# Ranks of a graph kernel's edge sort from five partly added one-hot rows: one addition on VectorE and 16 products on TensorE in place of four and four

## The reference, cut to what matters

```python
def _spmm(row, col, val, h, n_nodes):
    return jax.ops.segment_sum(val[:, None] * h[col], row, num_segments=n_nodes)
output_low = jax.nn.relu(_spmm(row, col, val_low, x @ weight_low, n))
output_high = jax.nn.relu(_spmm(row, col, val_high, x @ weight_high, n))
```

## Time and profile before

| | |
|---|---|
| time, median of 3 runs | 2471.05 us (2466.08 to 2477.81) |
| the profiled execution: its time | 2489.27 us |
| the profiled execution: its span | 2487.5 us |
| PE busy, products | 1724.4 us (69%), 9081 instructions |
| DVE busy | 1253.1 us (50%), 3123 instructions |
| ACT busy | 895.6 us (36%), 2606 instructions |
| POOL busy | 1376.2 us (55%), 1351 instructions |
| mean granted clock of TensorE | 0.833 of full speed |

### The profile page before, as it was taken

How to read it: one execution, slowest core, us unless ns; L and a number is a source line. 1 busy time by engine, 2 the same in 40 slices (tenths; PEclk the granted TensorE clock), 3 DMA queues, 4 the chain that set the end, 5 groups by cost and what they waited for, 6 DMA issues and landing times.

```text
span 2487.5 us, 30925 instructions
## 1 busy us (share of the span) xinstructions
PE 1724.4 (69%) x9081; PEld 1439.1 (58%) x9081; DVE 1253.1 (50%) x3123; ACT 895.6 (36%) x2606; POOL 1376.2 (55%) x1351
## 2 busy tenths in 40 slices
PE   4788886998845257775776777777677577577672
PEld 3566665787734146665665566666566466456562
DVE  8899986899752133333333332333333333333336
ACT  2667664787643022222222222222222222222223
POOL 3377774777776554545556455455455555555600
PEclk9899986999967668987888888888788788788886
DMA  3121101111100532323223223222222222222203
GB/s 90 46 54 38 48 13 36 38 55 54 38 5 5 126 80 69 79 68 78 70 69 84 68 73 74 67 73 72 66 75 73 72 72 76 77 70 69 85 9 103
DMA packets 206265, 156.60 MB, mean 63 GB/s; under 512 B 143354, under 2 KB 177676, under 8 KB 206092
## 3 DMA queue, kind: packets, MB, share of 16 engines
q0 software_dynamic: 55232, 113.59, 16.3%
q1 hardware_dynamic: 150860, 40.90, 7.4%
HBM read 139.76 MB, written 14.64 MB: 62 GB/s over the span
## 4 chain that ended last, share of the span: by engine, by line
PE 48%; issue 25%; ACT 8%; DVE 8%; POOL 7%; another core or an unknown queue 4%; DMA 1%; SPq 0%; DVEq 0%; ACTq 0%; POOLq 0%
PE bank L1514 46%; POOL sorted_records L647 6%; ACT arena L1308 1%; ACT base L1308 1%; ACT side L1308 1%; PE bank L1789 1%; POOL arena L664 1%; ACT arena L1429 1%; ACT side L1505 1%; DVE arena L807 1%; ACT arena L1433 1%; ACT arena L1312 1%; DVE arena L732 0%; ACT base L1354 0%
## 5 line engine op out<-in xcount | busy, mean ns | idle before, releaser
L1514 PE MATMUL bank<-arena 128*128 128x128 f32 (+3 forms) x6320 | 1305.4, 360 | 524.0 <-issue 434.5
L1514 PEld LDWEIGHTS bank<-arena 128*128 128x128 f32 (+1 forms) x6320 | 1098.1, 205 | 710.9 <-issue 547.5
L664 POOL DMA_INDIRECT arena<-xn_rows,arena x852 | 830.1, 974 | 740.5 <-SPq L558 460.5
L647 POOL DMA_INDIRECT sorted_records<-arena x448 | 522.3, 1166 | 249.5 <-issue 142.4
L1172 DVE CUSTOM_DVE_ANT_0 arena<-arena 128x256 f32<-128x256 f32 x98 | 37.8, 422 | 399.9 <-ACT arena L1438 363.1
L1177 DVE SCALAR_TENSOR_TENSOR att_prod<-sg,att_neg 128x9 f32<-128x9 f32 x49 | 8.5, 173 | 361.3 <-issue 319.6
L1124 DVE TENSOR_TENSOR arena<-arena 128x640 f32<-128x640 bf16 (+1 forms) x204 | 164.0, 804 | 41.9 <-DVE arena L1118 14.0
L1118 DVE SCALAR_TENSOR_TENSOR arena<-io,arena 128x320 bf16<-128x320 f32 (+1 forms) x204 | 97.7, 479 | 146.7 <-issue 65.4
L1476 ACT ACTIVATE arena<-bank 128x256 f32<-128x256 f32 x49 | 18.8, 383 | 401.5 <-remote 278.9
L1514 PE MATMUL bank<-arena,base 128*128 128x128 f32 (+3 forms) x766 | 119.8, 290 | 17.3 <-ACT base L1312 8.9
L807 DVE TENSOR_TENSOR arena<-arena 128x1280 f32<-128x1280 bf16 x84 | 120.6, 1488 | 18.7 <-remote 17.8
(11 more groups left out here) (306 smaller groups left out, 1875.5 us busy)
## 6 DMA issues: line engine op xcount, KB each, us to landing
arena<-xn_rows,arena POOLq DMA_INDIRECT x852
arena<-in_x SPq DMA_DIRECT2D x24, 512.0 KB
sorted_records<-arena POOLq DMA_INDIRECT x448
xn_rows<-arena SPq DMA_DIRECT2D x12, 512.0 KB
arena<-xn_rows SPq DMA_DIRECT2D x12, 512.0 KB
out<-base SPq DMA_DIRECT2D x4, 1024.0 KB
arena<-in_L_ffn_w SPq DMA_DIRECT2D x2, 1024.0 KB, 6.3
arena<-sorted_records SPq DMA_DIRECT2D x54, 32.0 KB
```

The costliest lines, as they stand in the source:

```text
L647: pool.indirect_dma_start(rec_dram, bass.IndirectOffsetOnAxis(ap=idx[0:PR, par, u:u + 1], axis=0), stage_rec[0:PR, par, u * 8:(u + 1) * 8] ...
L664: pool.indirect_dma_start(gring[:, c % GR, :], None, xn_dram, bass.IndirectOffsetOnAxis(ap=rring[:, c, 3:4].bitcast(I32), axis=0)).then_in ...
L1514: return pe.matmul(out_, lhsT, rhs, start=start, stop=stop, **kw)
```

## The change

`sum_hots` keeps its first addition alone, so `many` holds five rows for each group, each the sum of two one-hots. `ranks` applies the same weights to each of the five rows in turn, so that PE adds them up in PSUM: 5 products of 294 columns with `before`, 5 of 196 and 5 of 98 with `ones_b`, and the one of `diag`. `many_set` counts once for a batch instead of four times.

```diff
@@ -743,12 +743,6 @@
                 H = GS // 2
                 with nc.allow_low_precision(reason="whole numbers up to ten"):
                     dve.tensor_tensor(many[:, :, :, :], h[:, :, 0:H], h[:, :, H:GS], ALU.add).then_inc(S("many_set"), 1)
-                    dve.wait_ge(S("many_set"), 4 * g + 1)
-                    dve.tensor_tensor(many[:, :, 0:2], many[:, :, 0:2], many[:, :, 2:4], ALU.add).then_inc(S("many_set"), 1)
-                    dve.wait_ge(S("many_set"), 4 * g + 2)
-                    dve.tensor_tensor(many[:, :, 0], many[:, :, 0], many[:, :, 1], ALU.add).then_inc(S("many_set"), 1)
-                    dve.wait_ge(S("many_set"), 4 * g + 3)
-                    dve.tensor_tensor(many[:, :, 0], many[:, :, 0], many[:, :, 4], ALU.add).then_inc(S("many_set"), 1)
 
             def find_ties(g):
 
@@ -1516,14 +1510,17 @@
 
             def ranks(g):
 
-                pe.wait_ge(S("many_set"), 4 * g + 4)
+                pe.wait_ge(S("many_set"), g + 1)
                 wait(pe, S("idx_ready"), 1 if isinstance(g, int) and g == 1 else g - 1)
                 R = bank[0][:, 0:RANKS]
                 mm(R, ones_f[0:NB, :], diag[0:NB, :].unsqueeze(1).to_broadcast([NB, GROUPS, NB]), True, False, skip_group_check=True)
-                mm(R, before[:, :], many[:, :, 0, :], False, False, skip_group_check=True)
+                H = GS // 2
+                for j in range(H):
+                    mm(R, before[:, :], many[:, :, j, :], False, False, skip_group_check=True)
                 for s in range(GROUPS - 1):
-                    ins = mm(R[:, (s + 1) * NB:], ones_b[:, :], many[:, s:s + 1, 0, :].to_broadcast([P, GROUPS - 1 - s, NB]),
-                             False, s == GROUPS - 2, skip_group_check=True)
+                    for j in range(H):
+                        ins = mm(R[:, (s + 1) * NB:], ones_b[:, :], many[:, s:s + 1, j, :].to_broadcast([P, GROUPS - 1 - s, NB]),
+                                 False, s == GROUPS - 2 and j == H - 1, skip_group_check=True)
                 ins.then_inc(S("rank_ready"), 1)
```

## The result

Measured on one chip with the kernel before: 2508.61 us, the median of 4 executions (2485.8 to 2528.79), against 2468.57 us (2457.22 to 2477.81). The ratio is 1.0124, with an interval of 1.0091 to 1.0158: the change makes the kernel slower by 1.2%. The forecast was 2462 us, with a range of 2444 to 2482, and slower had a chance of 0.13. It is on the wrong side of no change, and outside the range.

A forecast was written before the change was run, and what follows sets the result against it. DVE was taken to set the kv slots, then PE, the fold's DVE-PE chain, POOL and PE again. Terms -11.1 - 2.2 + 1.0 + 3.1 - 1.1 - 2.2 + 4.1 = -8.4 us gave 2462 us, range 2444 to 2482.

The forecast's parts named there:

- What PE's own gaps cost: PE's pauses in scatter-only stretches: 24 more instructions in a batch of some 300 cost nothing, up to 20 us for the range.
- Rival C: Gaps on PE grow with instruction count; ranks of four batches pay about 0.7 us per added product: 2493 us, chance 0.15.
- The kv slots: DVE sets these first-stage slots; ten of them lose 1.11 us each, 11.1 us off, L745's starts 23.3 us apart.
- The 12 products: Added products in ranks on PE cost only their columns: 1.04 us per batch at full clock, 2.0 at half clock.
- The mix slots: 1.04 us added against 1.11 saved: no gain, about 1.3 us wait before the pick of ranks, round 21.4 us as before.
- the fold: Chain of DVE and PE in turn after the PE-bound stretch; the removed additions lie on it: 1.1 us off.
- the PE-bound piece: From 309.05 to 354.41 us PE sets the chain; three ranks fall to it: 3.1 us on.
- the end: End of the first stage, from 641.57 us, PE's chain through ranks: three rounds, 4.1 us on.
- POOL's batches after the fold: Scatter batches that POOL sets from 416 us: 24.2 us apart instead of 24.45, 2.2 us off over 11 batches.
- Rival A: All savings reach the end; POOL regains 1.11 us per batch it sets, 12 us: 25 us off, 2446 us, chance 0.20.
- The 0.2 us a batch: Small bf16 additions on DVE hold up POOL's scatters by this much; 2.2 us off over 11 batches.
- Rival B: Kv slots pass to POOL or PE at once, giving some 0.5 us each: no change, 2469 us, chance 0.20.

The follow-up runs named there:

- chip I: The first pair: the change against the kernel before, 2508.61 us against 2468.57, ratio 1.0124.
- chip V: Fourth group, against before at 2486.09 us: the change 1.0190, twelve two-column products 1.0104, less DVE work 1.0052, both edits together 1.0160.
- chip IV: Third group, against before at 2467.63 us: the change 0.9984, zero products of full widths 1.0018, two-column products 1.0026, less DVE work 0.9983.
- the DVE part: Kernel before with half the columns left out of each kv variance sum, 1.1 us less DVE per kv slot: 0.9961, 0.9983 and 1.0052 on three chips.
- chip III: Second group, against before at 2486.24 us: the change 1.029 by medians, three additions with rows 0 and 4 1.0112, 48 two-column products 1.0876.
- chip II: First group, before at 1990.70 us: four kernels with one engine's part of the change or half of it, 0.9961 to 1.0005; the change not run.
- Two rows: The change with three additions on DVE, rows 0 and 4 left for PE, three products more per group than before: 2531.79 us, 1.0112 of before.
- three rows: The change with two additions on DVE, rows 0, 1 and 4 left for PE, six products more per group than before: 1991.60 us, 1.0005 of before.
- its two parts: Kernel before with 12 zero products of 272, 196 and 98 columns in ranks, 0.9985; kernel before with half of each kv variance sum, 0.9961.
- empty products: Kernel before with 12 zero products of two columns added to each group's ranks: 0.9998, 1.0026, 1.0104 and 0.9993 of before on four chips.
- 48 products: Kernel before with 48 zero products of two columns added to each group's ranks: 2710.50 us, 1.0876 of before.

## Why the prediction was wrong

**The step that failed** is "What PE's own gaps cost", a term that I took at nothing, with up to 20 us for the range. On chip I the kernel is 40.0 us slower where the sum had 8.4 us less, so the term is 48 us short (40.0 + 8.4). On chip V it is 56 us by the first gather: 43.8 us later, where the change's execution on chip IV, which has no such stretches in its kv slots, has it 12.4 us earlier; both figures compare chips. Rival C had the sign in the profile, more gaps on PE between products of the same kind, with a chance of 0.15, and 2493 us for it, a loss of 34 us before the 12.3 us gained; it was short in size and wrong on the place. I looked for the gaps where the trace of before showed them, at 355 and 700 us, and priced each product that falls into one. What the runs show is that such stretches come where none was: in kv slots, from 150 or 200 us on, of some 4 to 13 us, in four of them on chip I (from about 204, 237, 275 and 331 us). And it is not the products alone that bring them: the DVE part by itself, which I had counted as pure gain, has them on chip V. A cost that depends on what is already there cannot be bounded by the gaps that are there. Nor is it all idle time: of the 57.6 us by which the first stage grew on chip I, 18 us are PE's idle time on issue, and some 21 us are PE busy for longer than its products explain (50.5 less 29), at a granted clock of 0.86 for 0.89. Why PE runs so in these stretches stays open.

**What held, in the execution without such stretches in its kv slots (chip IV).** The kv slots: 23.25 us, forecast 23.3. The 12 products: 1.03 us in the kv slot of chip V (1.29 less the 0.26 that a pair and its leader took before, 221.76 to 221.89 being half of it), forecast 1.04. The mix slots: 1.25 us of waiting where 0.23 was, forecast 1.3, and a round of 21.31, forecast 21.4. The sum: 12.4 us to the first gather, forecast 8.4; which of the smaller terms (the fold, the PE-bound piece, the end) has the 4 us the runs do not tell apart. The second stage is not touched, as forecast: on chip III its start and the end of the program have moved by 70.0 and 70.5 us. One sign failed even here: POOL's batches after the fold were to be 24.2 us apart, and 12 of them take 292.9 us (409.2 to 702.1), 24.4 for each, for 24.45. In the chances a small sum is off: all of A and a third of the forecast's 0.45 are 0.35, not 0.37.

**Rival A** (POOL relieved by 12 us) falls. A scatter takes as long as before on the mean, in the kernel before (first row, chip I) and in the change on chip IV (columns: busy us, mean ns, idle ahead):

```profile
L647 POOL DMA_INDIRECT sorted_records<-arena x448 | 522.3, 1166 | 249.5 <-issue 142.4 <-DVE arena L825 76.8 <-ACT arena L1328 30.2
```

```profile
L647 POOL DMA_INDIRECT sorted_records<-arena x448 | 526.3, 1175 | 232.9 <-issue 138.6 <-DVE arena L819 56.8 <-ACT arena L1322 37.4
```

1166 and 1175 ns, on two chips; on chip I the change has 1136, in slots that are longer and in which DVE stands idle more. The 12 us of the upper bound would be some 70 ns off each scatter of its 11 batches, or 27 off the mean of all (estimates: 1.11 us over 16, times 11/28), and are not there on chip IV. So the rule of the Trainium skill ("SBUF — State Buffer", "SBUF: two separate sides"), as I had taken it to hold for these additions in full, gave too much. The 0.2 us a batch of the forecast is too small to be seen in these means, but the trace of before bears it out: the 22 scatters beside which DVE ran nothing but the small additions and the cast behind them took 1155 ns on the mean, the 74 beside which it ran nothing 961.

**Rival B** falls as well: on chip IV the kv slots are 23.25 us without a new wait.

**The rule on fetches.** The Trainium skill, "Runtime: NRT & Kernel Launch", section "Instruction fetch mechanics", says that instructions come in blocks of 256 and that crossing is mostly hidden. The queue's count of packets agrees with the first half: 84 before, 87 with 672 more instructions (336 products and their weight loads), 95 with 2688 more.

```profile
q8 instruction: 84, 1.38, 0.2%
```

```profile
q8 instruction: 95, 1.56, 0.2%
```

By the second half such fetches would cost next to nothing, and the runs do not speak against it, since the stretches are not fetches as far as the traces show. In the change on chip V queue 8's 87 packets take 97 us together, while PE's idle time on issue is near 500; of its 389 gaps of 0.3 us and more on issue only 6 overlap a packet, and in the stretch from 185.5 to 197.6 us shown above no packet runs. A packet takes as long on either kind of chip (1.08 us on the mean on chip II, 1.07 on chip III).

So shown is that on chip V each part of the change costs by itself and both together what their product says, and that PE's stretches go with it. What makes the stretches is not shown, nor why some executions on chip IV are free of the loss. That PE is short of supply in them is my reading of the single products at equal steps, not a measurement. Every time here comes with a recorded span and clock, so that the recording itself has a part in the stretches is not ruled out either.

A version that beats both kernels did not come out of this. Two rows lost 1.1% on chip III, three rows changed nothing on chip II, and three rows on a chip of the other kind were not tried; nor was the change itself on a chip of 1990 us, where its two parts would multiply to a gain of 0.5% (0.9985 x 0.9961, an estimate).

## What to carry to other kernels

Where the profile shows PE idle on "issue" between products of one kind, its instructions are a resource of their own: an added product can cost more than its columns, and so can a shorter round of another engine. The gaps already there are no bound for it, and a single part measured alone is none either: on chip V empty products alone gave 1.0104, the whole change 1.0190. Trading a few DVE operations for many small products can then be a bad trade even when the columns hide. And time a change of one per cent on more than one chip: here one kernel gave 0.998 and 1.019 of before on two chips that run the kernel before within 1% of each other.

## What the runs showed of the hardware

Two kinds of chip, by this program: before takes 2468 to 2486 us on four of the six, and 1990 us on two. The first stage differs by some 40 us (first gather at 822.8 us in the kernel before on chip III, at 783.7 with 12 more products on chip II), the second by some 457. Busy times from 1300 to 1700 us, in the kernel before on chip III, then with 12 narrow products on chip II:

```profile
sum 400.00, PE 280.59 PEld 238.18 DVE 139.92 ACT 98.95 POOL 210.35; mean PE 280.59 PEld 238.18 DVE 139.92 ACT 98.95 POOL 210.35
```

```profile
sum 400.00, PE 341.23 PEld 291.59 DVE 202.07 ACT 138.91 POOL 306.48; mean PE 341.23 PEld 291.59 DVE 202.07 ACT 138.91 POOL 306.48
```

In the same 400 us POOL does 306 us of work instead of 210. The chain of work that ended last is, in these 400 us, PE's for 67.1% and "issue" for 28.4% on chip III, and the gathers' for 54.4% on POOL and 18.8% on DMA on chip II. So the program bound by PE on one kind of chip is bound by the gathers on the other. What makes a chip the one or the other no run tells; as each of these chips was used for one group only, a lasting property and a passing condition of a chip are not told apart.

The second surprise is the late handover: in the stretches ACT starts on PE's result 9.4 us (183.20 to 192.58) and, with 48 products, 14.0 us (164.94 to 178.98) after PE's record has the last product run, with "remote" as the releaser, which names no instruction. Where there is no stretch it follows at once: in the mix slot of chip IV the products end at 547.40 (546.59 + 0.81), and ACT's copy starts at 547.43.

```profile
546.59 0.81 PE L1508 MATMUL bank<-arena,ones_b 128*128 128x196 bf16 x10
...
547.43 0.42 ACT L1312 ACTIVATE arena<-bank 128x294 f16<-128x294 f32 x1 [2.16 <-PE bank L1508]
```

So it is not only that products come late there: either the end of those already run is seen late, or PE's record, whose ends are modelled, has them too early. No run tells which.
